# Attention: a batch's pair of row scatters goes out behind the signal of the next batch's scores

## The reference

```python
x = x + _L0_xattn_ref(_layernorm(x, axis=-1), ctx_1024, ctx_1024, ...)
x = x + _L0_ffn_ref(_layernorm(x, axis=-1), L0_ffn_Wg, L0_ffn_W1, L0_ffn_W2)
x = x + _L1_xattn_ref(_layernorm(x, axis=-1), ctx_1024, ctx_1024, ...)
x = x + _L1_ffn_ref(_layernorm(x, axis=-1), L1_ffn_gate_w, ...)
return x
```

## Time and profile before

| what | value |
|---|---|
| device time, median of 3 runs | 693.52 us (693.27 to 696.43) |
| span of the profiled execution, first to last instruction | 763.9 us |
| PE, DVE, POOL, ACT busy in the span | 88%, 69%, 66%, 54% |
| chain that ended last, by engine | PE 50%, POOL 17%, issue 12%, DVE 8%, ACT 5% |

### The profile page before, as it was taken

The page is one execution under the profiler, slowest core; times in us unless marked ns, Lnnn a source line. Parts: engine busy times, 40 slices in busy tenths (PEclk is TensorE's granted clock), DMA queues, the critical chain, the costliest instruction groups (busy, mean ns, idle before and its releaser), DMA issues.

```text
span 763.9 us, 21054 instructions
## 1 busy us (share of the span) xinstructions
PE 671.5 (88%) x7092; PEld 546.5 (72%) x7092; DVE 523.5 (69%) x1515; ACT 415.8 (54%) x1158; POOL 504.9 (66%) x837
## 2 busy tenths in 40 slices
PE   8799998888876999999979999888888668788797
PEld 7567666665646999999957776666667568778787
DVE  5489988888663446555358898888886555555556
ACT  5477767654542434444447777656547445555563
POOL 5975788577564678877677778777667635455451
PEclk9899999999997999999979999999989989899999
DMA  5470000001331522343110101111211312222264
GB/s 166 124 305 2 17 27 27 27 30 36 137 99 48 160 70 81 97 127 89 46 36 29 30 26 40 54 37 37 66 34 37 89 51 77 61 75 72 75 232 152
DMA packets 45406, 57.78 MB, mean 76 GB/s; under 512 B 11379, under 2 KB 37142, under 8 KB 44630
## 3 DMA queue, kind: packets, MB, share of 16 engines
q1 hardware_dynamic: 36086, 38.17, 16.6%
q0 software_dynamic: 8640, 17.97, 7.1%
q10 hardware_dynamic: 576, 0.29, 0.1%
HBM read 33.82 MB, written 22.08 MB: 73 GB/s over the span
## 4 chain that ended last, share of the span: by engine, by line
PE 50%; POOL 17%; issue 12%; DVE 8%; ACT 5%; another core or an unknown queue 4%; DMA 2%; SPq 1%; DVEq 0%; POOLq 0%; ACTq 0%
POOL results L1625 9%; PE ptp L1349 8%; PE M L1366 7%; PE ptp L2078 6%; PE S L1326 5%; PE S L2059 5%; PE S L1330 3%; PE ptp L1352 3%; POOL xi L1618 2%; POOL rows L626 2%; PE M L1374 2%; PE M L1418 2%; PE S L2065 1%; SPq L707 1%
## 5 line engine op out<-in xcount | busy, mean ns | idle before, releaser
L626 POOL DMA_INDIRECT rows<-out_rows,posi x128 | 126.9, 991 | 50.1 <-issue 32.1
L806 ACT ACTIVATE pT<-ptp 128x512 f32<-128x512 f32 (+1 forms) x192 | 95.1, 525 | 97.7 <-PE ptp L1349 87.0
L1929 POOL DMA_INDIRECT results<-early,xs x71 | 69.0, 971 | 68.4 <-DVE early L2001 50.9
L1064 DVE TENSOR_REDUCE mx<-S 128x16 f32<-128x1232 f32 x64 | 91.3, 1427 | 18.3 <-PE S L1330 16.4
L1625 POOL DMA_INDIRECT results<-early,xi x71 | 75.9, 1069 | 40.5 <-DVE early L1687 35.1
L1065 DVE TENSOR_TENSOR pr<-S,mx 128x1232 f32<-128x1232 f32 x64 | 92.3, 1442 | 2.2
L1724 PE MATMUL S<-first_w,early 128*128 x568 | 77.2, 279 | 3.0 <-DVE early L1687 1.5
L1714 PE MATMUL S<-early,w1s 128*128 128x128 f32 x568 | 76.9, 279 | 0.6 <-ACT early L1659 0.6
L1366 PE MATMUL M<-pT,vm 128*32 128x128 f32 (+1 forms) x2048 | 74.7, 283 | 1.1 <-ACT pT L806 0.6
L1349 PE MATMUL ptp<-cst,pr 128*128 128x128 f32 x512 | 74.0, 290 | 0.0
L1724 PEld LDWEIGHTS S<-first_w,early 128*128 128x128 f32 x568 | 69.5, 193 | 5.9 <-issue 5.7
(11 more groups left out here) (221 smaller groups left out, 1527.9 us busy)
## 6 DMA issues: line engine op xcount, KB each, us to landing
xs<-rows SPq DMA_DIRECT2D x142, 66.0 KB
first_w<-in_e_W SPq DMA_DIRECT2D x2, 2048.0 KB, 8.2
swap<-results SPq DMA_DIRECT2D x32, 128.0 KB
first_w<-results SPq DMA_DIRECT2D x6, 512.0 KB
rows<-out_rows,posi POOLq DMA_INDIRECT x128
x_res<-in_x SPq DMA_DIRECT2D x1, 1536.0 KB, 8.4
W1r<-in_e_W SPq DMA_DIRECT2D x1, 1536.0 KB, 10.8
out_x<-x_res SPq DMA_DIRECT2D x3, 512.0 KB, 2.7
```

The source lines that it names most:

```text
L626: nc.gpsimd.indirect_dma_start(rows[:, :], bass.IndirectOffsetOnAxis(posi[:, k, n:n + 1], 0), out_rows[:, ring_slot(groups, n), k, :], Non ...
L806: nc.scalar.activation(pT[0:rows_of, G * r:G * r + count, :], ptp[q % 2][0:rows_of, 0:count, :], ACT.Exp, scale=SCALE)\
L1064: do(V.tensor_reduce(mx[:, :].rearrange("p (g j) -> p g j", g=G), sc, AX.X, ALU.max))
```

## The change

Up to step 30, a step that has scatters no longer sends them at its end. The next step does, after its keys and before its padded values, behind a wait for `s_ready` to reach k+2, which is the scores of batch k+1. The wait for `pv_done` ahead of the scatters falls away there. Steps from 31 on are as before.

```diff
+        def late(k):
+
+            return k < B - 1 and len(sends.get(k, ())) > 0
+
...
             for n in range(keys_made(k - 1), keys_made(k)):
                 keys(n)
+            if late(k - 1):
+                wait(pool, s_ready, min(k + 2, B))
+                for n in sends[k - 1]:
+                    scatter(n)
             for n in (0, 1) if k == 0 and not rope else (k + 1,):
                 if k >= 0 and live(n):
                     padded_values(n)
...
+            if late(k):
+                yield k
+                continue
             if sends.get(k) and 1 <= k <= B:
                 pool.wait_ge(pv_done, k)
             for n in sends.get(k, ()):
                 scatter(n)
```

## The result

The changed kernel takes 727.07 us (median of 4 runs, 725.38 to 728.54), the kernel before 694.49 on the same chip: a ratio of 1.046, 95% interval 1.044 to 1.048. It is slower by 32.6 us, where 9.7 had been forecast.

What follows compares the result with a forecast made beforehand. No engine was full; waits between engines set the step length. Layer 0 at 0, layer 1's loop +6.4 and its end +4.3 gave +10.7 on 763.9 us, times 0.908: +9.7, 703 us (698 to 710), range 690 to 716.

Steps and rivals of the forecast that it cites:

- The base of the sum: Both layers: the earlier trace, span 763.9 us, with scatter steps of 5.91 us in layer 0 and 6.19 in layer 1.
- the prize: Both layers: moving pairs behind the transposes frees first exponentials, 0.61 us a step at most; 12 us and 11 us.
- the factor 0.908: Whole kernel: unprofiled runs of 693.52 us over the span of 763.9, used to turn span into run time.
- No signal of PE is held by a pair: Rival, both layers: late exponentials have another cause, no prize, layer 0 about +6; 16.7 us, 709 us; chance 0.08.
- the held signals: Scatter steps: a pair being issued delays PE's signals up to 0.61 us; later ones in layer 0 cost 6 us.
- its 10.7: Whole kernel: the forecast loss against the span, 0 + 6.4 + 4.3 us, giving +9.7 us in runs.
- The closed loop of layer 1: Steps 14 to 26: POOL's query and PE's scores wait in turn; 13 turns of 86.9 us against 80.5, +6.4.
- wake-up: POOL after the fresh wait for scores, ahead of the pair: taken as 0.27 us, upper bound 0.78.
- late factors: Layer 0: factors of `norms` reach ACT late behind the pair at every second step, 0.6 us each, 6 us.
- the 5.6: Layer 0: the prediction is wrong if steps there fall well under 5.6 us.
- The end of layer 1: Four more scatters and padded values ahead of `norms` of step 32 delay ACT's router rows: +4.3 us, between 0 and 5.3.

Runs made afterwards that it cites:

- the second trace: The kernel before, unchanged, profiled a second time: 695.82 us, span 694.0.
- e5: The change in layer 1 alone, with POOL waiting for the scores of the batch before instead of the next batch's: 698.53 us, 1.004 against the kernel before.
- e8: The change in layer 0 alone, with the factors of `norms(k + 1)` moved ahead of the late pairs of an odd step: 706.04 us, 1.017 against the kernel before.
- e9: The change in layer 0 alone, with both the factors of `norms` and the padded values ahead of the late pairs: 703.38 us, 1.010 against the kernel before.
- e2: The change in layer 1 alone, layer 0 keeping the old place: 714.08 us, 1.029 against the kernel before.

## Why the prediction was right in sign and too small

**The base of the sum and the prize: the step that failed.** The prediction took the earlier trace rows as normal steps, though it saw that the span was 70 us longer than the runs, and spread that over everything by the factor 0.908. The profiler alone does not lengthen a run so: the second trace has a span of 694.0 us for a run of 695.82. It also shows that the excess was not spread evenly: steps without scatters have the same length in both, steps with scatters lose 13.3 and 8.0 us in the first, and 41 of the 70 us lie behind layer 1's last transposes (763.9 less 571.38 against 694.0 less 542.87). So the prize of 12 and 11 us, read from the earlier trace rows, did not exist, and the loop was compared with steps of 6.19 us that were really 5.74. The rival "No signal of PE is held by a pair", with a chance of 0.08, had the right premise. The Trainium skill, SBUF — State Buffer, section "Who interferes with whom", says that PE and ACT never wait on anyone; the second trace agrees (0.69 us). That rival's price, 709, still stood on the old base. Without the prize and the held signals, and with the loop set against 73.9 us (below), the prediction's own terms give 6 + 13 + 4.3 = 23 us: this one step is 13 of the 20 us between its 10.7 and the 30.8 of the sum redone.

**The closed loop of layer 1: right, to a per cent.** The changed kernel's timeline, an odd step of POOL and PE's scores:

```profile
496.68 0.45 POOL L605 TENSOR_TENSOR qT<-swap 128x128 f32<-128x128 f32 x1
...
497.19 0.80 PE L1337 MATMUL S<-first_w,qT 32*128 32x308 f32 x8 [1.23 <-POOL qT L605]
...
497.92 0.47 PE L1341 MATMUL S<-bandb,identb 64*64 64x308 bf16 x8
...
498.69 1.05 POOL L630 DMA_INDIRECT rows<-out_rows,posi  x1 [1.55 <-PE S L1341]
...
500.04 0.96 POOL L630 DMA_INDIRECT rows<-out_rows,posi  x1 [0.30 <-issue]
...
501.03 0.41 POOL L584 TENSOR_TENSOR vm<-raw,cst 128x128 f32<-128x128 f32 x1
...
501.39 0.29 POOL L588 TENSOR_TENSOR vm<-raw,cst 128x64 f32<-128x64 f32 x1
...
503.15 0.46 POOL L605 TENSOR_TENSOR qT<-swap 128x128 f32<-128x128 f32 x1
...
503.66 0.80 PE L1337 MATMUL S<-first_w,qT 32*128 32x308 f32 x8 [1.23 <-POOL qT L605]
```

From query to query 6.47 us, priced at 6.46: scores from 497.19 to the end of the masks at 498.39, wake-up 0.30 (taken as 0.27), pair 2.31 (2.32), padded values 0.65 (0.66), then results and query. The 13 turns take 87.5 us (first transposes from 457.17 to 544.68), priced at 86.9. In the second trace of before the same steps take 73.9 (444.93 to 518.86), where the prediction set 80.5. So the term is +13.6, not +6.4, and nearly the whole miss of this term is the base. Single turns miss by more, and it cancels: the last takes 5.74 us, priced at 4.96. e5 shows that the wait closes the loop: without it these steps take 73.4 us.

**Layer 0: right cause, wrong place and size.** The prediction let late factors cost 0.6 us at every second step. Behind one pair they are late: in batches 12 to 24 ACT waits 12.3 us for them, before 4.3, and the first exponentials of batches 14, 16, 18, 20 and 24 come 0.2 to 1.0 us late. But in the same steps another loss of the old order went, which the prediction had not priced (PE's scores wait 0.6 us for DVE's subtractions, before 2.5), and in sum they cost nothing: 62.4 us against 63.2, or 5.2 a step, well under the 5.6 that the prediction had named as a sign of being wrong. The price lies where the plan sends twice in a step, which the prediction overlooked: batches 24 to 31 take 47.8 us (149.40 to 197.21) against 36.3 (150.23 to 186.51), +11.5. What it named, factors behind scatters, is shown by the 5.07 us of ACT's wait; the padded values, shown by e8 and e9, it did not name as a wait for layer 0. Up to 6.0 of the 11.5 us are PE at a lower clock behind these waits (last section).

**The end of layer 1: right path, half the price.** It forecast +4.3 by way of the factors of step 32 and ACT. The steps outside the 13 turns give back 2.4 us, and the last scatter comes 8.6 us later against the last transposes. The chain of the changed kernel goes by that path: ten scatters, the factors, and ACT's router rows of 579.76 after 8.45 us of wait. The power of these factors starts 11.8 us behind the last transposes, before 3.3, so 8.5 later, where the prediction took 5.3 less 1.0 of idle time. Four more scatters and the padded values are 5.6 of it; the other 2.9, which it lacked, are that the run of scatters starts later against the last transposes (at 564.20 for 566.61, before at 537.59 for 542.87). That the factors cause the rest of the delay is read from the chain and the waits, not shown by a run that moved everything ACT needs. From batch 13's transposes to the last scatter POOL is busy for 82.57 + 27.32 = 109.9 us of 142.4 in the second trace of before, and for 76.16 + 33.40 = 109.6 of 162.2 after the change. It does the same work with 20 us more idle time.

**The sum, redone.** Layer 0: 10.7 in the steps and 0.2 to the last scatter. Layer 1: 13.6 in the loop, -2.4 in the steps before and behind it, 8.6 to the last scatter. Together 30.8 of the 32.6 us; 1.8 are in none of these stretches. What lengthened the first profiled execution stays open: none of the later traces has such steps again.

## What to carry to other kernels

Before a profiled execution is read for waits, its span is set against the runs; where they differ by a tenth, the kernel is profiled again and the sum made against the trace that agrees. Ask of an engine off the chain what others need of it where its work piles up: what stands behind its late instructions comes late, and when one such thing is moved ahead the next one is waited for (factors and padded values in layer 0, factors and a memset in layer 1). And a wait on work that itself needs the waiting engine's next instruction but a few turns a queue into a loop, whose price is the plain sum of its parts.

## What the runs showed of the hardware

The same program had PE's signal 0.61 us late behind a pair in one execution and prompt in the next; span 763.9 and 694.0 us. The granted clock fell where the steps of layer 0 grew long: in the changed kernel it is 1.00 on average in batches 12 to 24 and 0.88, a mix of the two levels of 1.2 and 2.4 GHz, in batches 24 to 31, three of whose steps are long, and where PE is busy for 39.54 of 47.81 us. In the second trace of before batches 24 to 31 have 1.00 and PE is busy for 33.57 us with the same products, 6.0 less (last row):

```profile
87.00:149.40 62.40, 60.33 (x862) 42.99 (x858) 59.53 (x171) 45.49 (x134) 49.44 (x89) 1.00 0.09 28
149.40:197.21 47.81, 39.54 (x484) 27.78 (x481) 35.45 (x108) 22.86 (x59) 30.94 (x52) 0.88 0.21 74
```
```profile
150.23:186.51 36.28, 33.57 (x485) 24.13 (x481) 34.87 (x107) 22.28 (x57) 28.46 (x48) 1.00 0.20 64
```

Long steps alone do not bring the lower clock: the loop of layer 1 kept 1.00 in the changed kernel (114.61 us) and had 0.94 in e2 (116.12 us).
